# Causal attention on Trainium2: the two heads of a pair side by side in one four-bank buffer, with the transposed copies shared by two engines

## The reference

```
q = jnp.einsum('bsd,hqd->bhsq', x, w_q)
k = jnp.einsum('bsd,hqd->bhsq', x, w_k)
v = jnp.einsum('bsd,hvd->bhsv', x, w_v)
scores = jnp.einsum('bhsq,bhtq->bhst', q, k)
masked = jnp.where(causal, -jnp.inf, scores)
weights = jax.nn.softmax(masked / jnp.sqrt(jnp.float32(dq)), axis=-1)
out = jnp.einsum('bhst,bhtv->bhsv', weights, v)
cat = out.transpose(0, 2, 1, 3).reshape(b, s, -1)
return jnp.einsum('bsf,df->bsd', cat, w_o)
...
x = x + _L1_attn_ref(_layernorm(x, axis=-1), L1_attn_w_q, L1_attn_w_k, L1_attn_w_v, L1_attn_w_o)
```

## Time and profile before

| | us |
|---|---|
| median of 3 runs | 2679.04 (2679.01 to 2681.19) |
| profiled execution, its span | 2679.4 |
| PE busy in it | 2371.3 (89%) |
| DVE busy | 1672.6 (62%) |
| ACT busy | 1028.8 (38%) |
| mean granted TensorE clock | 0.926 of 2.4 GHz |

### The profile page before, as it was taken

The page is one execution under the profiler, slowest core; times in us unless marked ns, Lnnn a source line. Parts: engine busy times, 40 slices in busy tenths (PEclk is TensorE's granted clock), DMA queues, the critical chain, the costliest instruction groups (busy, mean ns, idle before and its releaser), DMA issues.

```text
span 2679.4 us, 41498 instructions
## 1 busy us (share of the span) xinstructions
PE 2371.3 (89%) x13282; PEld 1474.1 (55%) x13282; DVE 1672.6 (62%) x4404; ACT 1028.8 (38%) x1645; POOL 159.4 (6%) x272
## 2 busy tenths in 40 slices
PE   4479999965999899999999988998975998968698
PEld 3323333334677566666666656776653676744576
DVE  7788988856333576776767664333447436666566
ACT  1136767731444344344444423443322333322033
POOL 4211111140000000000000000000000000000000
PEclk8679999985999899999999998999987898989789
DMA  5010000000000000000000000001000000000000
GB/s 195 12 64 24 27 23 27 19 1 1 1 0 0 0 1 1 0 0 0 0 0 0 0 1 1 0 0 58 0 0 0 1 0 1 0 1 0 0 1 16
DMA packets 20814, 31.95 MB, mean 12 GB/s; under 512 B 5785, under 2 KB 11938, under 8 KB 19970
## 3 DMA queue, kind: packets, MB, share of 16 engines
q1 hardware_dynamic: 20738, 31.00, 3.4%
HBM read 26.40 MB, written 4.19 MB: 11 GB/s over the span
## 4 chain that ended last, share of the span: by engine, by line
PE 68%; DVE 8%; issue 1%; ACT 1%; DVEq 0%; ACTq 0%; POOL 0%; POOLq 0%
PE ps L270 17%; PE ps L258 16%; PE ps L466 9%; PE ps L478 5%; PE ps L493 5%; PE ps L863 2%; PE ps L503 2%; PE ps L445 2%; PE ps L202 1%; PE ps L251 1%; PE ps L442 1%; DVE xn L188 1%; PE ps L735 1%; PE ps L898 1%; DVE stat L139 1%
## 5 line engine op out<-in xcount | busy, mean ns | idle before, releaser
L270 PEld LDWEIGHTS ps<-l_w,arena 128*128 128x128 f32 x4096 | 535.9, 192 | 250.8 <-issue 235.3
L270 PE MATMUL ps<-l_w,arena 128*128 128x128 f32 x4096 | 543.2, 276 | 4.4 <-ACT arena L295 4.4
L258 PE MATMUL ps<-xnT,l_w 128*128 x1024 | 532.0, 606 | 0.0
L352 DVE SCALAR_TENSOR_TENSOR acc<-ps,comb,acc 128x128 f32 x768 | 216.2, 344 | 471.6 <-PE ps L270 469.4
L295 ACT ACTIVATE arena<-ps,l_b 128x512 f32<-128x512 f32 x384 | 263.6, 687 | 400.9 <-PE ps L258 400.9
L1755 DVE TENSOR_REDUCE arena<-ps 128x1 f32<-128x512 f32 x512 | 325.4, 684 | 38.3 <-PE ps L1542 38.3
L591 ACT ACTIVATE arena<-ps,arena 128x128 f32<-128x128 f32 (+7 forms) x256 | 188.3, 738 | 353.5 <-PE ps L478 315.4
L1685 ACT ACTIVATE arena<-ps 128x1024 f32<-128x1024 f32 x256 | 252.4, 1022 | 129.0 <-PE ps L1559 128.6
L466 PE MATMUL ps<-arena 128*128 128x512 f32 (+3 forms) x768 | 287.0, 492 | 1.6 <-ACT arena L591 0.8
L653 DVE COPY arena<-ps 128x512 f32<-128x512 f32 (+3 forms) x384 | 195.9, 547 | 135.6 <-PE ps L478 133.1
L644 DVE TENSOR_REDUCE arena<-ps 128x1 f32<-128x128 f32 (+7 forms) x256 | 187.6, 754 | 50.0 <-PE ps L469 44.7
(11 more groups left out here) (314 smaller groups left out, 2330.8 us busy)
## 6 DMA issues: line engine op xcount, KB each, us to landing
arena<-s_parts_q SPq DMA_DIRECT2D x96, 48.0 KB
arena<-s_parts_k SPq DMA_DIRECT2D x96, 48.0 KB
l_w<-in_l_w SPq DMA_DIRECT2D x2, 2048.0 KB, 14.2
l_w<-in_l_w SPq DMA_DIRECT2D x4, 1024.0 KB, 12.6
s_parts_q<-arena SPq DMA_DIRECT2D x2, 768.0 KB, 4.2
s_parts_k<-arena SPq DMA_DIRECT2D x2, 768.0 KB, 4.9
arena<-arena SPq DMA_DIRECT2D x96, 2.0 KB
x<-in_x SPq DMA_DIRECT2D x4, 256.0 KB, 3.6
```

The lines of the kernel that those rows point to most:

```text
L258: pe.matmul(k.ps[:, i % 2, :], w.w1[:, e, f * P:(f + 1) * P], k.xnT[:, bass.ts(g, GW)], start=True, stop=True).then_inc(s.hidden_mm.sem, 1)
L270: ins = pe.matmul(k.ps[:, 2 + e % 2, j * P:(j + 1) * P], w.h[:, i % 2, j * P:(j + 1) * P], w.w2[:, e, f, :], start=(f == 0 and j == 0), st ...
L352: ins = dve.scalar_tensor_tensor(acc, k.ps[:, 2 + e % 2:3 + e % 2, j * P:(j + 1) * P], k.comb[:, bass.ds(g * GT + j, 1), e], acc, ALU.mult ...
```

## The change

- The twelve units of one head become six units of both heads: (0, 3), (1, 2), (4), (5), (6), (7). The score matmuls of head h contract over 64 partitions on row tile (64h, 0) and go to banks 2h and 2h + 1, so that one unit fills all four banks; the loop alternates between the heads chunk by chunk. The masks stay matmuls over the full array, first those of head 0, then those of head 1.
- PE computes the scores of unit u + 1 after both heads' exponentials of unit u. The transposes of head 0 (turn h = 0) and of head 1 come one after the other through banks 4 and 5; ACT copies head 0's out, DVE head 1's.
- The output projection runs for both heads on two row tiles, head 0 into bank 7, head 1 into bank 6; its weights come from a slice that POOL copies. q and o hold both heads without zeros, in one copy each instead of two.
- y is added straight to x. acc's clearing and x += acc go, and the statistics of x for the next norm are taken at the end of this stage instead of the start of the next.

The diff, cut to its core (removed lines that stand in the printed functions above are mostly left out):

```diff
-    UNITS = [(h, qts) for g in ([(0, 3), (1, 2)], [(4,), (5,), (6,), (7,)]) for h in range(2) for qts in g]
+    UNITS = [(0, 3), (1, 2), (4,), (5,), (6,), (7,)]
     U = len(UNITS)
-    FIRST = 4
...
+    FIRST = 2
...
+        pool.wait_ge(s.y_mm, p * 8)
+        pool.tensor_copy(s.wb[:, 2, :], w.wo[:, bass.ts(p, P)]).then_inc(s.wo_slice, 1)
...
-        for i, qt in enumerate(qts):
...
+        for i, qt, _, width in s.spans(u):
             for c in range(0, width, GW):
                 n = min(GW, width - c)
-                last = c + n == width
...
+                for h in range(2):
+                    rows = slice(64 * h, 64 * h + 64)
+                    pe.matmul(k.ps[:, 2 * h + i + c // GW, 0:n], s.q[rows, b, qt * P:(qt + 1) * P],
+                              s.kT[rows, b, c:c + n], start=True, stop=c + n < width,
+                              tile_position=(64 * h, 0), skip_group_check=True)
+        for h in range(2):
+            for i, qt, _, width in s.spans(u):
+                n = (width - 1) % GW + 1
+                ins = pe.matmul(k.ps[:, 2 * h + i + (width - 1) // GW, n - P:n], k.ident_bf[:, :], k.future[:, :],
+                                start=False, stop=True, skip_group_check=True)
+            ins.then_inc(s.scores, 1)
+
+    def turn(f, u, h, first):
         for i, (_, kt, m, at) in enumerate(s.quads(u)):
-            if not (first and u == 0):
...
+            if h == 1:
+                pe.wait_ge(s.probsT_a, 2 * (f * U + u) + (i + 1))
+            elif not (first and u == 0):
+                pe.wait_ge(s.probsT_v, 2 * (f * U + u) + (i - 1))
             for j in range(m):
                 ins = pe.transpose(k.ps[:, 4 + i, j * P:(j + 1) * P],
-                                   s.p[:, u % 2, at + j * P:at + (j + 1) * P], k.ident[:, :])
+                                   s.p[:, 2 * (u % 2) + h, at + j * P:at + (j + 1) * P], k.ident[:, :])
             ins.then_inc(s.probsT_ps, 1)
...
-        pe.wait_ge(s.probsT, f * (2 * U) + 2 * (s.FIRST, U)[g])
+        done = 2 * (f * U) + 2 * (s.FIRST, U)[g]
+        pe.wait_ge(s.probsT_a, done)
+        pe.wait_ge(s.probsT_v, done)
         if not first:
-            pe.wait_ge(s.o_out, f * 2 + g)
...
+            pe.wait_ge(s.y_used, f * 4 + 2 * g)
+        pe.wait_ge(s.kv_out, f * 4 + (3 + g))
...
-        ins.then_inc(s.o_mm, 1)
...
+                if kt == kts - 1:
+                    ins.then_inc(s.o_mm, 1)
+
+    def output(n, pair):
         pe.wait_ge(s.o_out, n + 1)
-        if not first:
...
+        pe.wait_ge(s.wo_slice, pair + 1)
         for j in range(GT):
-            ins = pe.matmul(k.ps[:, 7, j * P:(j + 1) * P], s.o[:, h, j * P:(j + 1) * P],
...
+            for h in range(2):
+                rows = slice(64 * h, 64 * h + 64)
+                ins = pe.matmul(k.ps[:, 7 - h, j * P:(j + 1) * P], s.o[rows, j * P:(j + 1) * P],
+                                s.wb[rows, 2, :], start=True, stop=True, tile_position=(64 * h, 0))
+                if j == GT - 1:
+                    ins.then_inc(s.y_mm, 1)
...
             for u in range(U):
-                if u < U - 2:
...
+                pe.wait_ge(s.probs, 2 * (f * U + u) + 2)
+                if u < U - 1:
+                    scores(f, b, u + 1)
                 elif not end:
-                    scores(f + 1, 1 - b, u + 2 - U, f * U + (u + 1))
...
+                    scores(f + 1, 1 - b, 0)
                 if u == 0 and not begin:
                     values(f - 1, 1 - b, 1)
-                if u == s.FIRST:
+                if u == 1 and not end:
+                    pe.wait_ge(s.q_out, 2 * f + 3)
+                    project("k", 0, p + b, 1 - b, 7)
+                if u == 2:
                     values(f, b, 0, first=begin)
-                turn(f, u, begin)
+                if u == 3 and not end:
+                    pe.wait_ge(s.q_out, 2 * f + 4)
+                    project("k", 1, p + b, 1 - b, 7)
+                if u in (4, 5) and not end:
+                    if u == 4:
+                        pe.wait_ge(s.y_used, 4 * f + 2)
+                    else:
+                        pe.wait_ge(s.kv_out, 4 * f + 7)
+                    project("v", u - 4, p + b, 1 - b, 7)
+                turn(f, u, 0, begin)
+                if u == 0 and not end:
+                    pe.wait_ge(s.kv_out, 4 * f + 4)
+                    if b == 1:
+                        pe.wait_ge(s.slices, 2 * p + 4)
+                    project("q", 0, p + b, 1 - b, 7)
+                if u == 1 and not begin:
+                    if not end:
+                        pe.wait_ge(s.kv_out, 4 * f + 5)
+                    output(2 * f - 1, before)
+                if u == 2 and not end:
+                    if begin:
+                        pe.wait_ge(s.kv_out, 5)
+                    else:
+                        pe.wait_ge(s.y_used, 4 * f)
+                    project("q", 1, p + b, 1 - b, 7)
+                if u == 3:
+                    if not end:
+                        pe.wait_ge(s.kv_out, 4 * f + 6)
+                    output(2 * f, p)
+                turn(f, u, 1, begin)
...
+        act.activation(s.q[:, b, g * GW:(g + 1) * GW], k.ps[:, bank, :], ACT.Copy, scale=s.SCALE)\
+            .then_inc(s.q_out, 1)
+
+    def exp(f, b, u, first=False):
         for h in range(2):
-            rows = slice(64 * h, 64 * h + 64)
...
+            act.wait_ge(s.negmax, 2 * (f * U + u) + (h + 1))
+            if not (first and u < 2):
+                act.wait_ge(s.probsT_ps, 4 * (f * U + u) + (2 * h - 6))
+            src = k.ps[:, 2 * h:2 * h + 2, :].rearrange("p a b -> p (a b)")
+            for i, qt, at, width in s.spans(u):
+                ins = act.activation(s.p[:, 2 * (u % 2) + h, at:at + width], src[:, at:at + width], ACT.Exp,
+                                     bias=s.nm[:, u % 2, h, i:i + 1], accum_out=s.den[:, b * TB + qt, h:h + 1])
+            ins.then_inc(s.probs, 1)
+
+    def weights_out(f, u):
+        for i, (qt, a, m, _) in enumerate(s.quads(u)):
+            j = qt % GT
+            act.wait_ge(s.probsT_ps, 4 * (f * U + u) + (i + 1))
+            act.activation(s.pT[:, 0, a:a + m, j * P:(j + 1) * P],
+                           k.ps[:, 4 + i, 0:m * P].rearrange("p (i q) -> p i q", q=P), ACT.Copy)\
+                .then_inc(s.probsT_a, 1)
+
+    def o_copy(n):
+        act.wait_ge(s.o_mm, 2 * n + 2)
+        if not (isinstance(n, int) and n == 0):
+            act.wait_ge(s.y_mm, 2 * n)
+        act.activation(s.o, k.ps[:, 6, :], ACT.Copy).then_inc(s.o_out, 1)
...
-                exp(f, b, u, begin)
...
+                early = u in (0, 2)
+                if not early:
+                    weights_out(f, u)
+                if u < U - 1:
+                    exp(f, b, u + 1, begin)
+                elif not end:
+                    exp(f + 1, 1 - b, 0)
+                if early:
+                    weights_out(f, u)
+                if u == 0 and not begin:
+                    o_copy(2 * f - 1)
+                if u == 2:
+                    o_copy(2 * f)
+                if u in (0, 2) and not end:
+                    q_copy(f + 1, 1 - b, u // 2, 7)
...
-    st.done(dve.memset(k.acc[:, :, :], 0.0))
...
-        _, qts = s.UNITS[u]
...
+        for h in range(2):
+            dve.wait_ge(s.scores, 2 * (f * U + u) + (h + 1))
+            src = k.ps[:, 2 * h:2 * h + 2, :].rearrange("p a b -> p (a b)")
+            for i, _, at, width in s.spans(u):
+                ins = dve.tensor_reduce(s.nm[:, u % 2, h, i:i + 1], src[:, at:at + width], AX.X, ALU.max, negate=True)
+            ins.then_inc(s.negmax, 1)
 
     def weights_out(f, u):
-        h, _ = s.UNITS[u]
         for i, (qt, a, m, _) in enumerate(s.quads(u)):
             j = qt % GT
-            dve.wait_ge(s.probsT_ps, (f * U + u) * 2 + (i + 1))
...
+            dve.wait_ge(s.probsT_ps, 4 * (f * U + u) + (i + 3))
+            dve.tensor_copy(s.pT[:, 1, a:a + m, j * P:(j + 1) * P],
+                            k.ps[:, 4 + i, 0:m * P].rearrange("p (i q) -> p i q", q=P)).then_inc(s.probsT_v, 1)
+
+    def add(n, tiles):
+        st.done(dve.reciprocal(s.rden[:, tiles:tiles + GT, :], s.den[:, tiles:tiles + GT, :]))
+        for h in range(2):
+            dve.wait_ge(s.y_mm, n * 2 + (h + 1))
+            if h:
+                dve.wait_ge(s.y_used, n * 2 + h)
+            for j in range(GT):
+                x = k.x[:, tiles + j, :]
+                ins = dve.scalar_tensor_tensor(x, k.ps[:, 7 - h, j * P:(j + 1) * P],
+                                               s.rden[:, tiles + j, h:h + 1], x, ALU.mult, ALU.add)
+            ins.then_inc(s.y_used, 1)
 
     def pair(p, first=False, last=False):
         for b in range(B):
             f, begin, end = p * B + b, first and b == 0, last and b == B - 1
             for u in range(U):
-                if u < U - 2:
...
+                if u < U - 1:
+                    negmax(f, u + 1)
                 elif not end:
-                    negmax(f + 1, u + 2 - U)
...
```

(57 more changed lines are left out.)

89 lines of the change are left out of this document (15 added, 74 removed).

## The result

The changed kernel takes **2724.44 us**, median of 4 runs (2719.69 to 2734.15), beside 2679.03 for the kernel before measured with it (2676.09 to 2681.19): a ratio of 1.0171, 95% interval 1.0148 to 1.0194. The forecast of slower was right; 2749 was 25 us too high. The profiled execution is the slowest of the four, 2734.15 us with a span of 2732.4, so its rows hold some 10 us more than the median.

What follows compares the result with a forecast made beforehand. PE was taken to bound the kernel, 42.2 us a pass; 37.2 of work plus 10.0 of waits give 47.2. +70 over 14 full passes, +4 for first and last, -4.6 at the end: +70 on 2679.4, 2749, range 2700 to 2815.

Steps and rivals of the forecast that it cites:

- PE's work: Causal stage, per pass of two heads: PE's own work becomes 37.2 us, 5.0 less.
- k's copy: Rounds 1 and 3: the output waits for DVE's k copy behind two reductions, 1.0 and 1.4 us.
- the sums: Rounds 2 and 4: values and v wait for DVE's sums, begun only after its copies, 1.4 and 1.2 us.
- the exponentials: Rounds 4 and 5: PE waits for ACT's exponentials, which run behind ACT's copies, 1.95 and 1.6 us.
- PE stays the bound: Rival, chance 0.21: the price is PE's work alone, 37.2 us a pass, about 2595 us.
- h1 trails h0 by one pass of the chunk: Scores on two row tiles: head 1 finishes later than head 0, so scores take 10.1 us a pass, not 15.5.
- the case without a trail: Packed tiles start some 4 ns apart: scores take 7.8 us, a pass 45.6, the kernel 2727.
- the rival given 0.07, the clock: PE's clock falls in the new waits: at mean 0.9, 37 us of work some 4 longer, 2809; chance 0.07.
- as walked: Main case, chance 0.65: passes from 44.4 us (kernel 2710) to 49 us (kernel 2774).
- One copy, one output, two sums make 4.7: Causal stage's end, ACT's copy of o to the statistics: 4.7 us in place of 9.3, so -4.6.
- POOL's four memsets: Four memsets on POOL, said to wait on nothing near the chain: priced at nothing.
- The changes of tiling: Eight added pairs of tiling changes a pass, six at scores, two at outputs: 8 x 0.2 = 1.6 us.

Runs made afterwards that it cites:

- experiments 4: Changed kernel with DVE's sums of rounds 1 and 3 put before its copies of the transposed quads: 2687.26 us, ratio 1.0032.
- 5: Changed kernel with ACT doing head 0's exponential, then the copies, then head 1's exponential in rounds 1, 3, 4 and 5: 2694.08 us, ratio 1.006.
- 7: Changed kernel with DVE's sums before its copies, k or v copy between the reductions, ACT's copies between the two exponentials: 2654.15 us, ratio 0.9912.
- experiment 1: Changed kernel with both heads' score matmuls on row tile (0, 0), head 1's own scores left out: 2835.82 us, ratio 1.0587.
- the kernel of 6: Changed kernel with head 0's transposed copies back on DVE, so that ACT has none: 2692.29 us, ratio 1.0053.
- Experiments 3: Changed kernel with extra matmuls, results overwritten, before the waits for the exponentials, two in round 4, one in round 5: 2707.66 us, ratio 1.0112.

## Why the forecast was right, and where its sizes were off

**The direction and its cause: shown.** PE's work fell by 6.3 us a pass (41.9 to 44.7 - 9.05 = 35.6) and the waits took back 9. At full clock a pass is thus 2.5 us longer than before. Where the forecast put them they are: k's copy 0.73 and 1.32 (forecast 1.0 and 1.4), the sums 1.79 and 1.45 (1.4 and 1.2), ACT's copies 0.36 and 0.25 (0.7 and 0.8), the exponentials 1.77 and 1.38 (1.95 and 1.6); 9.05 for 10.0. That they are single chains shows in experiments 4, 5 and 7, which take them away one after another with no engine's work changed. The rival "PE stays the bound" fell here.

**The step that was mis-sized is PE's work**, 37.2 for 35.6; the waits were 10.0 for 9.05. "h1 trails h0 by one pass of the chunk" made scores 10.1 us. From start to the next row they are 8.97 a pass with their changes of tiling, of which 7.7 are columns; experiment 1 has the trail at nothing. The trail had been read out of the 0.15 by which `values` exceed half, which fits the 0.2 of a change of tiling as well. The Trainium skill's "TensorE: Matmul & The Clock Gate", Part 3, which was held against it, had this right; its 2727 was the better number, though by a pass of 45.6 and with the clock at full. And an output is 1.09 from start to the next row, where 1.4 and a change of tiling, 1.6, were taken: its sixteen loads take 0.97 together, as eight did before, so the tiles load in pairs. The recorded 45.6 of the case without a trail, less 2 x 0.5 for the outputs, is 44.6 (an estimate from these rows) beside the 44.0 to 44.7 measured. The fourteen passes cost +33.4 in work and waits where +70 was forecast.

**What covered for that** is the rival given 0.07, the clock. It adds 28.7 us in the profiled execution and 16.8 between medians; the forecast's mechanism (37 us of work some 4 longer, at 0.9) was right in kind. In size it is 2.5 to 3.3 us in each of nine passes at about 0.93, 2.1 on average over the fourteen, whose mean clock is 0.95. So 2749 came near by luck, by two misses of opposite sign, and the case "as walked" and the clock rival hold together rather than one against the other.

**The ends.** "One copy, one output, two sums make 4.7": 4.3, so -5.0 for -4.6. For the first and last pass +2 each was taken. The first lost 6.3, with waits like those above and a fall of the clock near its end; the last gained 4.7 beside the end, half of it because the last `values` before took 8.24 in place of 5.81. POOL's four memsets, put at nothing because they "wait on nothing near the chain", were worth 3.0: nothing waited for them, but DVE's normalizations stood still beside them. This is read from the traces; no run took away the memsets alone. The stages ahead are unchanged: PE busy 763.50 us up to 916 at clock 0.90, beside 761.75 at 0.89.

**The changes of tiling** cost somewhat more than the 0.2 that was taken: 0.2 from the start of the scores to the next row, and some 0.1 in the turn before them (0.64 us for five tiles, 0.55 in the earlier trace rows). The drain that the Trainium skill states in "TensorEngine Tiling (Array Packing)", Key Properties, was thus no reason against the change.

**Open:** why the clock falls in some passes and not in others. Between 1170 and 1540 us the kernel of 6 has PE busy for 83% with no fall, that of 7 for 88% with falls (clock 0.98), the changed kernel for 82% at 0.93, so busy share alone doesn't decide. Experiments 3 and 5, which shorten or fill the waits for the exponentials, end the falls, so these waits have a part in it. But they aren't enough by themselves: in the changed kernel the first four full passes keep the full clock with the same waits (1.77 and 1.38) as those in which it falls (1.80 and 1.38). No run varied their place alone.

## What to carry to other kernels

When a change makes the busiest engine's work shorter by giving up a buffer, walk the round: each wait is one chain through the other engines' programs, and the order of instructions there decides, not their busy time. Then reorder before judging the change: here the same tiling is 1.7% slower in one order and 0.9% faster in another. A helper that takes over half of an engine's copies must not take them ahead of what the bound engine waits for.

## What was not expected of the hardware

- Two row tiles of f32 with 64 rows cost half in full: 1.99 against 3.70 us for 2 x 1024 columns, in whichever order the heads are issued (1.99 with one head's matmuls all behind the other's).
- Weight loads for two row tiles overlap: sixteen of 128 columns in 0.97 us.
- DVE stood still beside POOL's memsets: normalizations of 0.34 us took 1.7 to 1.9 where they started with or during a memset of 1.8 us, and all sixteen took 7.14 in place of 4.20.
- A clock that falls behind waits of 1.4 to 1.8 us, with PE busy for four fifths of the time, made work beside it up to 1.8 times as long (v 2.02 for 1.11), and three useless matmuls in the right place bought 17 us; where the waits were already short, they cost 7. The same waits left the clock at 1.00 or 0.99 in five passes of fourteen.
